# Seven early experts, x1 as float16 halves turned by DMA, and one order for the FFN steps

## What is computed

```python
x = layernorm(x + attention(x))            # 16 heads of 64, softmax over the causal keys and a null key
# FFN, N = 4096 tokens
scores = softmax(x @ wg.T)                 # 32 experts in 8 groups; the best 4 groups, in them the top 4 experts
pos = cumsum(one_hot(idx)) - 1             # place of a token in its expert, kept if pos < cap = 640
xe = x[buf_tok]                            # (32, 640, 128)
h = silu(xe @ w1) * (xe @ w3)
out = (h @ w2) * buf_w
y = scatter_add(out)
z = silu(x @ sw1) * (x @ sw3) @ sw2        # shared expert, all tokens
x = layernorm(x + y + z)
```

## Time and profile before

| | |
|---|---|
| runs | 974.48 us median of 3 (970.93 to 975.97) |
| profiled execution | span 977.5 us; the profile gives no other time of its own |
| TensorE busy | 859.0 us (88%) |
| VectorE busy | 654.3 us (67%) |
| ScalarE busy | 616.8 us (63%) |
| GpSimd busy | 673.5 us (69%) |
| mean granted TensorE clock | 0.943 |

### The profile page before, as it was taken

The page is one execution under the profiler, slowest core; times in us unless marked ns, Lnnn a source line. Parts: engine busy times, 40 slices in busy tenths (PEclk is TensorE's granted clock), DMA queues, the critical chain, the costliest instruction groups (busy, mean ns, idle before and its releaser), DMA issues. The chain is left out here.

```text
span 977.5 us, 25690 instructions
## 1 busy us (share of the span) xinstructions
PE 859.0 (88%) x9439; PEld 633.9 (65%) x9439; DVE 654.3 (67%) x2448; ACT 616.8 (63%) x1189; POOL 673.5 (69%) x580
## 2 busy tenths in 40 slices
PE   5789999999999999999999999766688888888654
PEld 2367777777777777777777777654465666666422
DVE  7757788987987987987987986836243434343217
ACT  3668889888888888888898787733132323233305
POOL 7656665699698699699689689346665555556636
PEclk9989999999999999999999999978798989899968
DMA  5787788645444454354354342016333323333147
GB/s 160 182 255 234 231 243 220 177 107 134 97 119 111 101 135 108 89 151 107 73 141 122 72 117 64 21 51 197 119 96 100 96 79 95 95 101 99 39 191 252
DMA packets 104428, 126.62 MB, mean 130 GB/s; under 512 B 22077, under 2 KB 65426, under 8 KB 103408
## 3 DMA queue, kind: packets, MB, share of 16 engines
q1 hardware_dynamic: 95408, 109.25, 40.8%
q0 software_dynamic: 8896, 15.74, 5.2%
HBM read 33.68 MB, written 41.58 MB: 77 GB/s over the span
## 5 line engine op out<-in xcount | busy, mean ns | idle before, releaser
L2289 POOL TENSOR_TENSOR PL<-PF,PH 128x1280 f16<-128x1280 f32 x121 | 317.8, 2626 | 107.2 <-ACT PH L1632 63.7
L1854 DVE CUSTOM_DVE_ANT_0 JUNK<-PS,M 128x256 f16<-128x256 f32 (+3 forms) x512 | 225.2, 485 | 39.5 <-PE PS L1265 35.8
L1626 ACT ACTIVATE PF<-PS 128x512 f32<-128x512 f32 (+1 forms) x384 | 192.8, 520 | 80.3 <-PE PS L1298 75.4
L2332 POOL DMA_INDIRECT y_rows<-BIG,Q x150 | 145.7, 972 | 99.3 <-ACT BIG L1551 57.4
L1632 ACT ACTIVATE PH<-PF 128x1280 f16<-128x1280 f32 x128 | 162.2, 1267 | 0.6
L2322 POOL DMA_INDIRECT xe_rows<-PAY,DEST x128 | 129.3, 1010 | 42.9 <-issue 27.7
L1291 PE MATMUL PS<-Q,K 128*128 128x512 f16 (+3 forms) x512 | 148.6, 300 | 9.2 <-DMA Q<-MROW 4.9
L1315 PE MATMUL PS<-VH,PH 128*128 128x65 f16 x1280 | 141.3, 195 | 13.0 <-DVE Y L1896 8.5
L1317 PE MATMUL PS<-VH,PL 128*128 128x65 f16 x1280 | 141.3, 194 | 1.2 <-issue 1.2
L1315 PEld LDWEIGHTS PS<-VH,PH 128*128 128x128 f16 x1280 | 119.6, 98 | 35.0 <-issue 24.5
L1316 PE MATMUL PS<-VL,PH 128*128 128x64 f16 x1280 | 141.3, 194 | 0.0
(11 more groups left out here) (252 smaller groups left out, 2027.5 us busy)
## 6 DMA issues: line engine op xcount, KB each, us to landing
K<-KH SPq DMA_DIRECT2D x128, 128.0 KB, 2.3
Q<-QH SPq DMA_DIRECT2D x128, 128.0 KB, 2.4
xe_rows<-PAY SPq DMA_DIRECT2D x20, 520.0 KB, 4.2
Q<-xe_rows SPq DMA_DIRECT2D x30, 325.0 KB
K<-KL SPq DMA_DIRECT2D x64, 128.0 KB, 2.3
Q<-QL SPq DMA_DIRECT2D x64, 128.0 KB, 2.3
y_rows<-PAY SPq DMA_DIRECT2D x16, 512.0 KB, 4.9
K<-in_L_ffn_w_dram SPq DMA_DIRECT2D x96, 64.0 KB
```

The lines of the kernel that those rows point to most:

```text
L1626: e.activation(PF[:, n % PBUF, c0:c0 + width], PS[:, k, 0:width], ACT.Exp).then_inc(s["c_exp"], 1)
L1854: e.tensor_tensor_reduce(JUNK[:, n_ttr % 2, 0:width], PS[:, base + ab, c0:c0 + width], M0[:, 512 - width:512], 1.0, -3e38, ALU.add, ALU.ma ...
L2289: e.tensor_tensor(PL[:, n % PBUF, :], PF[:, n % PBUF, :], PH[:, n % PBUF, :], ALU.subtract).then_inc(s["c_lp"], 1)
L2332: e.indirect_dma_start(out=y4[:, :], out_offset=bass.IndirectOffsetOnAxis(ap=XE[:, x_ % 6, k, 128:129].bitcast(I32), axis=0), in_=OUT[:, x ...
```

## The change

- `NA` is 7. Experts 0 to 6 take rows of the first seven batches only, and their part of the last batch becomes seven dense pieces. Their weights lie in sets of their own (`SETS`), loaded on SP in the last heads of attention, with the rows of experts 0 to 3 and six batches of x1.
- The plan puts their steps among the last unit's and the last batch's: expert 0's hidden product before the last head's values, the others' between the steps of routing, their y scatters with them on GpSimd's queue.
- x1 is written to DRAM as two float16 halves (high, and the rest), in `PAY` too; rows of an expert and batches of x1 are loaded with a transposing DMA, so no turn on TensorE and no copies by VectorE. The weights w1, w3 are split in two halves by ScalarE and VectorE. A hidden product or dense up is three float16 products: high by high, high by low, low by high.
- The number and weight of a row (8 bytes) come by a DMA of their own.
- All eight blocks of the shared expert are pieces of `DENSE` (31 in all): `LEAD` = 4 ahead of the loop, 2 behind it, 25 spread over the loop's 23 experts.
- Dense pieces have PSUM banks 5, 6, 7 to themselves, experts 0 to 4; the last batch's halves use one bank each.
- Batches 5 to 7 are routed with shorter pauses (`PAUSES_LATE`), and a scatter goes with each `place` in the last seven heads.

```diff
-NA = 2
-NS1 = 5
+NA = 7
+LEAD = 4
-DENSE = ([(SHARED, b) for b in range(NS1, NB)] + [(d, b) for d in range(ND) for b in range(NB)]
+DENSE = ([(SHARED, b) for b in range(NB)] + [(d, b) for d in range(ND) for b in range(NB)]
          + [(ND + j, NB - 1) for j in range(NA)])
+PAUSES_LATE = (10, 6, 3, 5, 2, 3, 3, 4)
...
+        if ms == NH - 3:
+            for j in range(4):
+                step("load set", j)
+            for b in range(6):
+                load_x1t(b)
+            for x_ in range(4):
+                step("load rows", x_)
...
             elif name == "values" and ms == NH + 1:
                 if ("yc", 4 * NB - 1, 0) not in marks:
                     next(last)
+                    into(0)
+                    step("times", 0)
                 values(ms - 2, args)
...
+    out_of_expert(0)
+    rows_out(0)
     next(last)
+    into(1)
     upto(0, "power")
     next(last)
+    step("times", 1)
     upto(1, "stats 1", True)
     upto(0, "normalize")
     upto(1, "power")
...
+    out_of_expert(1)
+    rows_out(1)
+    into(2)
     upto(0, "x1t")
     upto(1, "normalize")
+    step("times", 2)
     upto(0, "payi")
     upto(1, "x1t")
+    out_of_expert(2)
+    rows_out(2)
+    into(3)
     upto(0, "hot mask 0", True)
+    step("times", 3)
     upto(1, "payi")
+    out_of_expert(3)
+    rows_out(3)
+    into(4)
     for half, gen in enumerate(halves):
         for _ in gen:
             pass
+        step("times", 4 + half)
+        out_of_expert(4 + half)
+        rows_out(4 + half)
+        into(5 + half)
         left.extend((NB - 1, q, k) for q in range(*span(half)) for k in range(4))
         while left:
             scatter()
...
+    step("times", 6)
+    out_of_expert(6)
+    rows_out(6)
...
+    while piece < LEAD:
+        up(piece)
+        piece += 1
+    into(NA)
+    step("times", NA)
+    for x_ in range(NA, NE):
+        if x_ + 5 < NE:
+            step("load rows", x_ + 5)
+        if x_ + 4 < NE:
+            step("load ring", x_ + 4)
+        if x_ + 2 < NE:
+            step("ring split", x_ + 2)
...
+        if x_ + 1 < NE:
+            into(x_ + 1)
+            step("times", x_ + 1)
+        due = LEAD + (len(DENSE) - TAIL - LEAD) * (x_ - NA + 1) // (NE - NA)
+        if piece < due:
+            up(piece)
+            piece += 1
+        out_of_expert(x_)
+        rows_out(x_)
...
+        def three(out, halves, m, x_of, free):
+            high, low = halves[:, 0, 128 * m:128 * m + 128], halves[:, 1, 128 * m:128 * m + 128]
+            for o, n in free:
+                e.matmul(out(o, n), high, x_of(0, o, n), start=True, stop=False)
+                e.matmul(out(o, n), high, x_of(1, o, n), start=False, stop=False)
+            for o, n in free:
+                i = e.matmul(out(o, n), low, x_of(0, o, n), start=False, stop=True)
+            return i
...
-            e.dma_start(XE[:, x_ % 6, :, :], xe_e[expert(x_)]).then_inc(l_xe[x_ % 6], 16)
+            w.wait_ge(s_hid, 2 * (x_ - 5))
+            w.wait_ge(s_oc, 5 * (x_ - 5))
+            e.dma_start_transpose(XT[:, x_ % 6, :, :], xe_t[expert(x_)][:, 0:256]).then_inc(l_xe[x_ % 6], 16)
+            e.dma_start(XI[:, x_ % 6, :, :], xe_i[expert(x_)][:, :, 128:130]).then_inc(l_xe[x_ % 6], 16)
```

More of the change, by code:

```diff
@@ L474, in finish @@
         mark("ex", b, *half, by="c_aj")
-        for h in half:
-            step("payload", b, h)
-            mark("payx", b, h, by="c_aj")
-            mark("payi", b, h, by="c_pg")
+        if not whole:
+            rows(half[0])
         yield from wait(5)
@@ L482, in finish @@
             yield
+        if not whole:
+            low(half[0])
+            if half == (1,):
+                step("x1 store", b)
+                mark("xts", b, by="c_xts", n=16)
         dv("gate sum")
@@ L546, in last_unit @@
         yield
-        step("first out", pj_free[0])
+        step("first out")
         mark("wo", u, "first", by="c_pm")
@@ L562, in last_unit @@
         for half in (0, 1):
-            step("last out", half, (pj_free[1], (("xa", u, "first"),))[half])
+            step("last out", half)
             mark("wo", u, half, by="c_pm")
@@ L587, in load_x1t, with into, out_of_expert, rows_out @@
         step("load x1t", b)
-    def load_w(e_):
-        step("load w", e_)
-    def shared(b):
-        step("shared up", b)
-        mark("up", b, by="c_ph")
-        mark("silu", b, by="c_as")
-        yield
-        step("shared times", b)
-        mark("zt", b, by="c_dz")
-        yield
-        step("shared down", b)
-        mark("down", b, by="c_pz")
-        yield
-        step("shared add", b)
-        mark("z", b, by="c_dz")
-        yield
+    def into(x_):
+        if x_ < NA:
+            step("set split", x_)
+        step("hidden", x_)
+        step("silu", x_)
+    def out_of_expert(x_):
+        step("product", x_)
+        step("outs", x_)
+    def rows_out(x_):
+        for k in range(5):
+            step("rows out", x_, k)
+    begun = []
+    def down():
+        if begun:
+            i = begun.pop()
+            step("dense down", i)
+            step("dense add", i)
+    def up(i):
+        down()
+        for name in ("dense up", "dense silu", "dense times"):
+            step(name, i)
+        begun.append(i)
     todo = {}
@@ L769, in plan @@
         place(slow)
-    if ready and not left:
+    while ready or left:
         scatter()
-    while len(left) > 4:
-        scatter()
-    for b in range(NB - 1):
-        load_x1t(b)
-    for e_ in range(4):
-        load_w(e_)
-    step("load dense")
-    for x_ in range(NA):
-        step("load early rows", x_)
-    gate_free = (st_free[0], st_free[1])
+    for j in (4, 5):
+        step("load set", j)
+        step("load rows", j)
+    for x_ in range(NA, NA + 4):
+        step("load ring", x_)
+    load_x1t(6)
+    for j in range(6, NA + ND):
+        step("load set", j)
     halves = [finish(NB - 1, 0), finish(NB - 1, 1)]
@@ L819, in plan @@
     load_x1t(NB - 1)
-    for b in range(2):
-        next(parts[b])
-    for b in range(2):
-        next(parts[b])
-        next(parts[b])
-    step("early turn", 0)
-    next(parts[2])
-    next(parts[2])
-    step("early hidden", 0)
-    step("early turn", 1)
-    next(parts[3])
-    next(parts[3])
-    step("early product", 0)
-    next(parts[2])
-    next(parts[2])
-    step("early hidden", 1)
-    next(parts[3])
-    next(parts[3])
-    step("early product", 1)
-    next(parts[4])
-    next(parts[4])
-    step("first turn")
-    next(parts[4])
-    next(parts[4])
-    bank_end = [key for keys in (*st_free.values(), *mx_free.values(), *pj_free[:2], last_keys) for key in keys]
-    return steps, marks, {name: x.sem for name, x in c.items()}, bank_end, free
+    for x_ in range(6, NA + 5):
+        step("load rows", x_)
+    step("set split", SHARED)
+    step("times", 6)
+    out_of_expert(6)
+    rows_out(6)
+    for j in range(NA, NA + ND):
+        step("set split", j)
+    forms = list(range(len(WEIGHTS)))
+    step("ring split", NA)
+    step("ring split", NA + 1)
+    piece = 0
+    while piece < LEAD:
[10 more added lines that the diff above has]
+            step("ring split", x_ + 2)
+        for k in forms[0:2]:
+            step("form", k)
+        forms = forms[2:]
+        if x_ + 1 < NE:
[7 more added lines that the diff above has]
+        rows_out(x_)
+        while piece < due:
+            up(piece)
+            piece += 1
+    while piece < len(DENSE):
+        up(piece)
+        piece += 1
+    down()
+    return steps, marks, {name: x.sem for name, x in c.items()}
 def build(nc, x, Wq, Wk, Wv, Wo, null_k, null_v, logit_scale, wg, w1, w2, w3, sw1, sw2, sw3, out):
@@ L1509, in tensor @@
-        product(NE - 1)
-        for i in range(IN_LOOP, len(DENSE) + 1):
-            if i < len(DENSE):
-                dense_up(i)
-            if i > IN_LOOP:
-                dense_down(i - 1, 5 * (NE - 1) + 3)
+            elif name == "dense up":
+                dense_up(*a)
+            elif name == "dense down":
+                dense_down(*a)
         def begin(i):
@@ L1769, in vector @@
+            r.then_inc(s_dacc, 1)
         for name, *a in steps:
```

706 lines of the change are left out of this document (336 added, 370 removed).

## The result

The changed kernel takes 1024.39 us (median of 6) beside 972.7 for the kernel before (6 runs) on the same chip: ratio 1.0527, 95% interval 1.0464 to 1.0591. The forecast was 924 us, faster. The profiled execution has a span of 1012.0 us (its own time 1013.88), for 977.5.

The account below looks back on a forecast made before the run. GpSimd's 166 indirect DMAs at 1.276 us were to bound the kernel after attention: 659.3 + 211.8 + 2 + 5 + 5 + (150 - 146.7) = 886.4, plus 40.7 closing, 927.1 span, less 3.0: 924 us, range 902 to 947.

Parts of the forecast that it names:

- Splitting x1 in attention ... I take 0; bounds 0 and 8: Attention: two added VectorE instructions a batch, 2.4 us in 74, cost 0 us because TensorE sets the pace.
- I take the 35 steps fewer to be worth about that idle time: Routing of batches 5 and 6: shorter pauses recover about the 13.2 us of idle time before batch 6's first scatter.
- The first y scatter at 659.3: Expert 0, end of attention: last values at 653.4 plus hidden 3.4, product 2.2, copy 0.3; bounds 651 and 667.
- GpSimd reaches the last batch's first scatter only after 25 y scatters: Last batch's routing: that scatter comes at 691 at the earliest, so some 20 us of routing delay are free.
- rival 2: Last batch's routing is delayed by more than 20 us and GpSimd waits 15 more: 939 us, chance 0.11.
- The early waits: Early experts: GpSimd waits 5 us, for expert 1's product, bounds 0 and 10.
- The wait ahead of the loop: First loop expert: landing, load and products sum to 11.4 us, expert 6's scatters cover 6.4, a wait of 5.
- I take 150, the middle: Loop of 23 experts: 150 us against GpSimd's 146.7, between that and TensorE's 154 with lags; bounds 147 and 168.
- rival 1: TensorE still paces the loop, 7.05 us an expert, 162 us for 150: 936 us, chance 0.18.
- (3): Better, GpSimd has no wait at all and starts y scatters at 651: 907.5 us, chance 0.15.
- (4): Slower, transposing loads pace the loop, break-even at 8.7 us a load: over 975 us, chance 0.07.
- (5): No change: the early work only shifts GpSimd's idle time; chance 0.02.

Follow-up runs that it names:

- e2: The kernel before, plus VectorE writing the same 1024 payload elements once more twice a batch, with scatters waiting for it, batches 0 to 6: ratio 1.0299.
- e8: The changed kernel without the extra scatter at each place step of the last seven heads: ratio 1.0542 to the kernel before.
- e14: The changed kernel with the kernel before's pauses in batches 5 and 6 and without the last seven heads' extra scatters: ratio 1.0478 to the kernel before.
- e15: The changed kernel with x1's low half spread by ScalarE, expert 0 behind the last heads, old pauses, no extra scatters: ratio 1.0284 to the kernel before.
- e3: The changed kernel with experts 1 to 6 moved behind the last batch's routing and scatters: ratio 1.0579 to the kernel before.
- e10: The changed kernel without the four dense pieces ahead of the loop (LEAD 0): ratio 1.0616 to the kernel before.
- e11: The changed kernel with x1's low half spread by ScalarE, expert 0 behind the last heads, no dense pieces ahead of the loop: ratio 1.0478 to the kernel before.
- e12: The changed kernel, unchanged, on a quick chip: ratio 1.0569 to the kernel before.
- e16: As e15, with all seven early experts behind the last batch's routing and scatters and no dense pieces ahead of the loop: ratio 1.0161 to the kernel before.
- e13: The kernel before, unchanged, profiled again on a lagging chip, the kind where it took 972 to 980 us.
- e6: The changed kernel, unchanged, on a lagging chip: ratio 1.0461 to the kernel before.

## Why the prediction was wrong

The sum, term by term, against the profiled execution (lagging chip):

| term | forecast | measured |
|---|---|---|
| first y scatter | 659.3 | 696.4 |
| 166 GpSimd DMAs at 1.276 | 211.8 | 211.8 (same count, taken at the same pace) |
| waits in the early block | 5 | 3.35 + 2.05 + 4.77 + 3.04 = 13.2 |
| wait ahead of the first loop expert | 5 | 20.1 |
| loop over GpSimd's floor | 3.3 | 176 - 146.7 = 29.3 |
| small steps, other | 2 | 3.1 (the rest) |
| closing | 40.7 | 38.1 |
| span | 927.1 | 1012.0 |

- **"Splitting x1 in attention ... I take 0; bounds 0 and 8"** failed in size and in kind. It cost 20 us by 522 us and 25 by 603, where the shorter pauses have a part; e2, which has nothing else, takes 26 us longer. I counted busy time (2.4 us in 74 on an engine busy 83%) where the order on the queue counts: a wait for ScalarE, a stand behind GpSimd, TensorE idle, and then the lower clock. The end of that sentence ("if VectorE is late for the running maxima") named the mechanism and priced it 3 times too low.
- **"I take the 35 steps fewer to be worth about that idle time"** (13.2 us) failed: 3 us, and 8 lost in attention (e8, e14). The steps wait for one another's data and for engines that are full; leaving out pauses between them shortens little.
- **The first y scatter at 659.3** failed by 37: with attention and pauses as before it still comes at 671.8 (e15), 12.5 late. The sum counted from the last values, but expert 0 waits for its rows, and batch 6's last scatter ends at 658.9 in e15; in the first trace it ended at 666.7, where the prediction had "653 at the earliest". The chain from the rows was near: 11.5 us from the load to the first y scatter in e15 and 11.6 in e3, for the 4.7 + 3.4 + 2.2 + 0.3 = 10.6 of the sum, which left out silu and times, 1.5 us. In the profiled execution it took 16.2 (680.2 to 696.4).
- **"GpSimd reaches the last batch's first scatter only after 25 y scatters"** was right and decisive: 742.2, with routing ready. So the cover held (rival 2 wrong, though its sign, a first scatter later than 700, came: the sign did not tell it from a late start), but it was the wrong gain to look for: the kernel before starts that scatter at 669.7, and the change fills 16 us of idle GpSimd at best.
- **The early waits** came from y scatters that begin 9 to 11 us apart an expert, 3 us and more over the floor of 6.4, where I had priced one wait of 5. Behind the routing the same experts follow 6.4 us apart (e3), and GpSimd waits as long elsewhere. Which of the shared queues spaces them in front was not tried.
- **The wait ahead of the loop**, 11.4 less 6.4, was mis-sized: 15 us from the last scatter's end on quick chips, and 29 with lags (798.0 less 768.7). On quick chips the 4.7 from the hidden product on is what failed: 9.8, as the next expert's hidden product and a dense piece come before the product; without the pieces ahead it was no shorter (e10, e11). With lags a late release of 14.5 us and the pieces behind it came on top.
- **The loop, "I take 150, the middle"**: TensorE's work of 5.3 us a turn was right (123.5 us busy in e12 for 23 experts, 5.4). The bound of 147 was met on quick chips, where it gains nothing. In the profiled execution it is 176, worse than my bound of 168 and than rival 1's 162. The step that failed is that the lags keep their old proportion or less: they come at shorter intervals, y scatters wait 2.7 to 3.3 us for copies at most of them, and the ring does not take that up. Why they come sooner stays open. The last 23 experts took 183.4 us before (their first y scatter is issued at 753.4) and 176 after, a gain of 7.
- Of the 85 us between forecast and span, 37 lie ahead of the first y scatter, 8 in the early waits, 15 ahead of the loop and 26 in it.
- The closing and rivals 3 to 5 need no more than a line: the closing was right, no wait was saved (3), the loads land in 4.3 us for the break-even of 8.7 (4), and the time did change (5).

No version beats the kernel before. The best, e16, loses 1.6% on a lagging chip; its first scatter of the last batch is 11.5 us later than e13's (681.0 for 669.5), 5.7 of them the longer wait for the unnamed release, and its 23 loop experts take 186.7 us for e13's 181.4. Its cheaper operations are spent on more work there: 28 dense down products stand in that stretch, 18 dense pieces in e13's, and TensorE is busy 142.5 us for 146.1. The rest is open with the lags.

## What to carry to other kernels

Price an added instruction by its place in the queue: what it waits for, which operation of another engine it may stand behind, and who waits behind it, not by its share of the engine's idle time; a stall of 3 us on a TensorE at full clock costs 4. Before starting work early on the engine that bounds the end, compute when its first input lands and when the first work from it is ready, and compare that with when the engine now starts: here it was 2 us later (671.8 in e15, 669.5 in e13). And ask whether a pace is the kernel's or the chip's before building a gain on it.

## What the runs showed of the hardware

- A VectorE subtraction of two SBUF operands that meets a GpSimd operation of 2.62 us ended 0.3 to 1.1 us behind it, at 2.38 us for 1.21 and 1.58 for 0.41.
- The same kernel takes 905 us on some chips and 975 on others. Of the 57.5 us between the changed kernel's spans (1012.0 and e12's 954.5) 29 lie in the loop, where late releases behind TensorE's work come only on the slower chips: every 25.5 us in the kernel before, mostly every 15.5 in the changed one (15.7 and 23.3 in e6). The granted clock was 1.00 during such a wait (761 to 767 us in the kernel before). What releases late is not shown by name.
- A transposing load of 320 KB of float16 rows with a small one took the DMA queue to a share of 46.4%, a plain load of 325 KB to 24.1%, and landed in 4.3 us for 3.1. The Trainium skill (Advanced Engine Details and Errata, X-Bar Transpose (TRN2)) has it as fast as a regular one; here it was 1.2 us slower and cost the kernel nothing.
- Each of five ScalarE table loads in the early block took 1.28 us. From the start of the load to the start of the next function it was 1.30 us once and 2.3 to 2.8 four times:

```profile
712.50 1.28 ACT L1759 ACT_TABLE_LOAD   x1
713.80 0.23 ACT L1759 ACTIVATE PS<-LG 128x64 f32<-128x64 f32 x1
...
716.89 1.28 ACT L1591 ACT_TABLE_LOAD   x1
719.70 0.70 ACT L1591 ACTIVATE Y<-PS 128x640 f32<-128x640 f32 x1 [1.53 <-issue]
```

  The prediction took the smaller price. The second pair, in which the silu waited 1.53 us for nothing that the trace names, fits the 2.66 us a switch of the Trainium skill (ScalarE: Activation LUTs, What ACT_TABLE_LOAD costs), the first does not. As the routing kept its cover, it decided nothing.
